# Sort columns of a graph kernel: two-source grids replaced by one-source compares, column by column

## The reference

```
agg  = zeros(N, D).at[src].add(edge_attr)            # layer 0: a sum of edge rows by src
h    = relu(layernorm(x));  x = x + MLP([h, agg, attention(h, u)])
ht   = relu(relu(layernorm(x)) @ W1 + b1)            # layer 1
msg  = sigmoid(exp(w) * ht[src] + b)
fsum = segment_sum(msg, dst, N)                      # a sum of table rows (by src) by dst
out  = x + relu(normalise([ht, c(fsum)] @ Wn + bn))
```

## Time and profile before

| what | us |
|---|---|
| median of three executions | 2619.27 |
| span of the profiled execution | 2625.3 |
| DVE busy | 1911.2 (4995 instructions) |
| PE busy | 1974.8 |
| POOL busy | 1754.5 (1674 instructions) |
| DVE on line 1186, on line 1190 (two groups), on line 1182 (two groups) | 171.7, 166.4 + 165.9, 75.4 + 75.0 |

### The profile page before, as it was taken

How to read it: one execution, slowest core, us unless ns; L and a number is a source line. 1 busy time by engine, 2 the same in 40 slices (tenths; PEclk the granted TensorE clock), 3 DMA queues, 4 the chain that set the end, 5 groups by cost and what they waited for, 6 DMA issues and landing times.

```text
span 2625.3 us, 34327 instructions
## 1 busy us (share of the span) xinstructions
PE 1974.8 (75%) x8533; PEld 1372.0 (52%) x8533; DVE 1911.2 (73%) x4995; ACT 1320.0 (50%) x4349; POOL 1754.5 (67%) x1674
## 2 busy tenths in 40 slices
PE   1389974677867977877898676796897797898884
PEld 0256652445544644644587454564564555575553
DVE  1468882776787798788588578688688689663478
ACT  0145523444744743754436644564564474474565
POOL 1468887777777777777105777777777777777503
PEclk9689986788988998988999798999898999898998
DMA  9989978734643333333365543343333333344445
GB/s 380 280 176 194 195 136 193 179 100 112 163 118 101 107 99 101 105 101 101 106 200 209 180 119 99 111 113 109 111 112 109 110 111 112 111 137 137 118 137 162
DMA packets 182981, 371.10 MB, mean 141 GB/s; under 512 B 33292, under 2 KB 102054, under 8 KB 180213
## 3 DMA queue, kind: packets, MB, share of 16 engines
q0 software_dynamic: 93168, 219.39, 33.8%
q1 hardware_dynamic: 78423, 114.54, 13.5%
q10 hardware_dynamic: 11200, 35.00, 3.5%
HBM read 282.15 MB, written 99.74 MB: 145 GB/s over the span
## 4 chain that ended last, share of the span: by engine, by line
PE 41%; DVE 17%; DMA 12%; POOL 11%; issue 11%; ACT 4%; SPq 3%; DVEq 1%; ACTq 0%; POOLq 0%
PE bank L1514 39%; POOL store L703 10%; DVE agg L1259 7%; DMA store<-in_edge_attr,idx_all 5%; DMA store<-g_table,idx_all 4%; SPq L483 1%; DMA w1bT<-turned_scratch 1%; DVE hits L1186 1%; DVE cum L1143 1%; DVE store L1450 1%; ACT dist L834 1%; POOL agg_copy L677 1%; DMA agg<-in_x 1%; ACT oh L842 1%; ACT store L776 1%
## 5 line engine op out<-in xcount | busy, mean ns | idle before, releaser
L1514 PE MATMUL bank<-store,oh 128*128 (+2 forms) x4610 | 1253.5, 410 | 397.1 <-DMA store<-in_edge_attr,idx_all 115.9
L1514 PEld LDWEIGHTS bank<-store,oh 128*128 128x128 f32 (+1 forms) x4610 | 814.0, 192 | 732.7 <-issue 434.2
L1259 DVE TENSOR_TENSOR agg<-bank,agg 128x256 f32 x1845 | 773.4, 419 | 397.5 <-PE bank L1514 305.9
L703 POOL DMA_INDIRECT store<-g_table,idx_all x785 | 769.4, 980 | 245.9 <-issue 156.3
L842 ACT ACTIVATE oh<-dist 128x128 f32<-128x128 f32 x1845 | 494.7, 302 | 653.9 <-PE bank L1514 628.2
L703 POOL DMA_INDIRECT store<-in_edge_attr,idx_all x628 | 626.0, 997 | 194.3 <-issue 131.3
L834 ACT ACTIVATE dist<-iota,nloc_all 128x128 f32<-128x128 f32 x1845 | 583.1, 387 | 61.8 <-DVE nloc_all L1231 61.8
L677 POOL DMA_INDIRECT agg_copy<-agg x160 | 262.1, 1638 | 154.7 <-ACT agg L799 64.9
L1186 DVE TENSOR_TENSOR hits<-iota,ttab 125x628 f16<-125x628 f16 x360 | 171.7, 477 | 0.0
L1190 DVE TENSOR_TENSOR oh<-hits,v 125x628 f16<-125x628 f16 x360 | 166.4, 479 | 3.2
L1190 DVE TENSOR_TENSOR store<-hits,v 125x628 f16<-125x628 f16 x360 | 165.9, 480 | 3.3
(11 more groups left out here) (211 smaller groups left out, 1926.0 us busy)
## 6 DMA issues: line engine op xcount, KB each, us to landing
agg_copy<-store ACTq DMA_DIRECT2D x4, 6400.0 KB, 38.3
agg<-in_edge_attr SPq DMA_DIRECT2D x39, 512.0 KB, 5.0
agg_copy<-agg_copy POOLq DMA_DIRECT2D x16, 800.0 KB
store<-g_table,idx_all POOLq DMA_INDIRECT x785
store<-in_x SPq DMA_DIRECT2D x48, 256.0 KB, 4.7
store<-in_edge_attr,idx_all POOLq DMA_INDIRECT x628
pre_scratch<-store SPq DMA_DIRECT2D x25, 256.0 KB, 5.3
agg<-agg_copy SPq DMA_DIRECT2D x25, 256.0 KB, 6.8
```

Of the source, the lines that this page charges most:

```text
L703: gp.indirect_dma_start(out=store[:, at % RING * D:(at % RING + 1) * D], out_offset=None, in_=table_dram, in_offset=bass.IndirectOffsetOnA ...
L1259: dve.tensor_tensor(to, pt[n % TB][:, 0:D], to, ALU.add).wait_op(s_mm, n + 1, "sem-ge").then_inc(s_acc, 1)
L1514: return pe.matmul(o, l, r, start=start, stop=stop, skip_group_check=skip)
```

## The change

`COLUMN_OPS` goes from 4 to 3. `hit` is made by four `tensor_scalar` instructions, one per column (a row `counting` of 0, 1, 2, ... in f16 compared with one number per partition from `rtab`). The grid `tile_of` and its semaphore go: each half of `placed` is made by four `tensor_scalar` instructions, which compare `counting` with the partition's `ttab` and multiply with the partition's value in the same instruction. So a batch is 12 instructions of 128 or 158 columns in place of 4 of 512 or 628. The columns lie one behind the other, 158 (`TPAD`) apart, so that PE reads them without stride; buffers move accordingly. Since the column part has 120 atoms in place of 160 at the same planned weight, `spread_over` deals all atoms out anew over the same 146 steps and 40 blocks.

```diff
--- before.py
+++ after.py
@@ -54,6 +54,7 @@
 LOADS = 8
 NLOC = 160
 BOTH = NLOC + TILES
+TPAD = TILES + 1
 TREST = TILES - P
 TURN = 512 - P
 RING = 64
@@ -66,7 +67,7 @@
 
 BATCH = 4
 BATCHES = COLS // BATCH
-COLUMN_OPS = 4
+COLUMN_OPS = 3
 COUNT_ATOM = SEGS
 CC_ATOM = COUNT_ATOM + 3
 PLACE_ATOM = CC_ATOM + 5
@@ -165,6 +166,7 @@
         msk = sb("msk", [P, NWS * COLS], F16)
         cum = sb("cum", [P, NWS * COLS], F16)
         hits = sb("hits", [P, BATCH * TILES], F16)
+        counting = sb("counting", [P, TPAD], F16)
         hit1 = sb("hit1", [P, BATCH * P], F16)
         win = sb("win", [P, SORTS * COLS], F16)
         v1 = sb("v1", [P, SORTS * COLS], F16)
@@ -238,11 +240,10 @@
         ohv = oh[:, 0:OHS * SW].rearrange("p (k n) -> p k n", n=SW)
         distv = dist[:, :].rearrange("p (k n) -> p k n", n=SW)
         columns16 = oh[:, OHS * SW:].bitcast(F16)
-        hit = (columns16[:, 2 * BATCH * TILES:2 * BATCH * TILES + BATCH * P], hit1)
-        tile_of = hits
+        hit = (columns16[:, 2 * BATCH * TPAD:2 * BATCH * TPAD + BATCH * P], hit1)
         spare = store[:, RING * D:].bitcast(F16)
-        placed = tuple(t[:, 0:2 * BATCH * TILES].rearrange("p (v n) -> p v n", v=2) for t in (spare, columns16))
-        after = RING * D + BATCH * TILES
+        placed = tuple(t[:, 0:2 * BATCH * TPAD].rearrange("p (v n) -> p v n", v=2) for t in (spare, columns16))
+        after = RING * D + BATCH * TPAD
         jobtile = store[:, after:after + JT]
         pick = store[:, after + JT:after + 3 * JT].rearrange("p (a n) -> p a n", a=2)
         turned = store[:, after + 3 * JT:after + 3 * JT + 2 * P].rearrange("p (a n) -> p a n", a=2)
@@ -321,7 +322,7 @@
                                                      ("s_mask", "s_colcount", "s_colstart", "s_startstore", "s_startload"))
         s_pf, s_pfd = sem("s_prefix"), sem("s_placed")
         s_col, s_colmm, s_scat, s_dec = (sem(n) for n in ("s_col", "s_colmm", "s_scat", "s_dec"))
-        s_hit, s_code, s_lag = sem("s_hit"), sem("s_code"), sem("s_lag")
+        s_code, s_lag = sem("s_code"), sem("s_lag")
         s_node, s_pick, s_turn, s_nl = (sem(n) for n in ("s_node", "s_pick", "s_turn", "s_jobbias"))
         s_g = [sem(f"s_rows{b}") for b in range(SLOTS)]
         s_abs, s_oh, s_mm, s_acc = (sem(n) for n in ("s_abs", "s_oh", "s_mm", "s_acc"))
@@ -995,6 +996,7 @@
             dve.wait_ge(s_gi, CONSTS)
             pc.mark(dve.tensor_copy(iota1[:, :], dec_a[:, 0:SW]))
             pc.mark(dve.tensor_copy(iota2[:, :, :], dec_a[:, 0:JT].unsqueeze(2).to_broadcast([P, JT, 2])))
+            pc.mark(dve.tensor_copy(counting[:, :], dec_a[:, 0:TPAD]))
             pc.mark(dve.tensor_copy(iotac[:, :], dec_b[:, 0:2]))
             pc.mark(ts(low[:, :], tri[:, :], -1.0, 1.0, ALU.mult, ALU.add))
             pc.mark(dve.tensor_copy(ident16[:, :], ident[:, :]))
@@ -1166,29 +1168,18 @@
                 at = sig * BATCHES + batch
                 b = at % 2
 
-                def pairs(tab, c0):
-                    t = tab[K, c0 + batch * BATCH:c0 + (batch + 1) * BATCH].rearrange("p (a i) -> p a i", i=2)
-                    return lambda width: t.unsqueeze(2).to_broadcast([KP, BATCH // 2, width, 2])
-
-                def grid(t, width):
-                    return t.rearrange("p (a n i) -> p a n i", a=BATCH // 2, i=2)
-
-                def numbers(width):
-                    return iota2[K, 0:width, :].unsqueeze(1).to_broadcast([KP, BATCH // 2, width, 2])
-
+                c0 = batch * BATCH
                 if op == 0:
                     if at >= 2:
                         dve.wait_ge(s_colmm, at - 1)
-                    dve.tensor_tensor(grid(hit[b][K, :], P), numbers(P), pairs(rtab, 0)(P), ALU.is_equal)
-                elif op == 1:
-                    if at:
-                        dve.wait_ge(s_col, at)
-                    dve.tensor_tensor(grid(tile_of[K, :], TILES), numbers(TILES), pairs(ttab, 0)(TILES), ALU.is_equal).then_inc(s_hit, 1)
+                    for i in range(BATCH):
+                        ts(hit[b][K, i * P:(i + 1) * P], counting[K, 0:P], rtab[K, c0 + i:c0 + i + 1], None, ALU.is_equal)
                 else:
-                    v = op - 2
-                    dve.wait_ge(s_hit, at + 1)
-                    r = dve.tensor_tensor(grid(placed[b][K, v, :], TILES), grid(tile_of[K, :], TILES), pairs((v1, v2)[v], sig * COLS)(TILES),
-                                          ALU.mult)
+                    v = op - 1
+                    by = (v1, v2)[v][:, sig * COLS + c0:sig * COLS + c0 + BATCH]
+                    for i in range(BATCH):
+                        r = ts(placed[b][K, v, i * TPAD:(i + 1) * TPAD], counting[K, :], ttab[K, c0 + i:c0 + i + 1], by[K, i:i + 1],
+                               ALU.is_equal, ALU.mult)
                     if v:
                         r.then_inc(s_col, 1)
 
@@ -1617,14 +1608,9 @@
                 b = at % 2
                 pe.wait_ge(s_col, at + 1)
 
-                def column(t, a, i):
-                    return t.rearrange("p (a n i) -> p a n i", a=BATCH // 2, i=2)[:, a, :, i]
-
                 both = pS[:, 0:2 * NLOC].rearrange("p (v n) -> p v n", v=2)[:, :, 0:TILES]
-                for a in range(BATCH // 2):
-                    for i in range(2):
-                        r = mm(both, column(hit[b][K, :], a, i),
-                               placed[b][K, :, :].rearrange("p v (a n i) -> p v a n i", a=BATCH // 2, i=2)[:, :, a, :, i], False, False, True)
+                for i in range(BATCH):
+                    r = mm(both, hit[b][K, i * P:(i + 1) * P], placed[b][K, :, i * TPAD:i * TPAD + TILES], False, False, True)
                 r.then_inc(s_colmm, 1)
 
             def sort_atom(sig, a):
```

## The result

The changed kernel takes 2819.37 us (median of 4 runs, 2817.83 to 2830.08) against 2619.32 for the kernel before on the same chip: ratio 1.0777, 95% interval [1.0758, 1.0797]. It is slower, as forecast, but by 200 us and not by 100.

The account below looks back on a forecast made before the run. POOL's gathers bound the kernel before; after, DVE bounds the column parts. Six groups +84, groups 0 and 4 +16, adding DMAs -10, prologue +10: together +100 on 2619, say 2720 us, range 2620 to 2900.

Parts of the forecast that it names:

- `placed` at 0.17 us: DVE's batch: each of eight `placed` instructions costs 0.17 us, 1.37 us together, within 2.02 us a batch.
- The dearer reading: `placed`: second number per partition costs like the first, 2.54 us a batch; as rival (or no f16 gain) 2880 us, chance 0.18.
- The stall of 0.18 us per gather: Column parts: one-source DVE instructions wait for POOL, 0.18 us charged per gather, bounds 0 and 0.36.
- `hit` at 0.16: DVE's batch: each of four `hit` instructions costs 0.16 us, 0.65 us together.
- the f16 column at half price: DVE instructions: an f16 column costs half of an f32 column's 0.5 ns, so 128 columns take 0.03 us, 158 take 0.04.
- The gathers' excess: Gathers beside columns take 0.994 us, not 0.945; up to 32 us over eight sorts could come back.
- Prologue +10: Prologue: DVE gets 15 us more work and the last blocks are dense, costing 10 us, bounds -8 and +30.
- The order of atoms that I had charged nothing: LAG 5: PE's matmuls one atom behind the `hit` that waits for them; up to 3 us at a time, in the range only.
- The 7 us that I took off each group: Each group: the ring takes up about 7 us of the column part's 27 us excess over POOL's pace.
- The "-10" for the adding DMAs of groups 0 and 1: Groups 0 and 1: 16 adding DMAs that POOL issues now lie beside DVE's work, taking 10 us off.
- The rival "no stall": Column parts: instructions slip between POOL's, groups stay at 203 us, only the prologue counts: 2628 us, chance 0.12.
- a new releaser: Sign at POOL: gathers wait several us for PE, where such waits had been 0.3 us at the longest.

Follow-up runs that it names:

- The strip beside gathers: Strips of twelve DVE instructions per form behind the changed kernel's end, in quiet and beside 40 more gathers: 24 two-number instructions took 5.16 us quiet, 5.19 beside gathers.
- the version whose DVE isn't the bound: Changed kernel with planned column atom weight 0.56 for 0.42 and the second half of `placed` not computed: 2606.30 us, ratio 0.9936 to the kernel before.
- the pair with LAG 4: LAG 4 in place of 5 in the changed kernel and in the kernel before, second chip: 3004.29 us (ratio 1.0460) and 2874.73 us (1.0000).

## Why the prediction was off

Right in sign and in its main mechanism (DVE becomes the bound in the column parts and POOL waits), too small by half. Two large terms of the sum failed, in opposite directions, and a cost that I had put at nothing was not nothing.

- **`placed` at 0.17 us: wrong, 0.232.** This is the step that failed. I put the second number at nothing and gave instructions with two numbers the fixed part of 0.13 us that I had for one. The dearer reading stood among the bounds and the rivals; "both could be fetched together" was all that spoke against it. A batch is 2.51 us and not 2.02; over 320 batches beside gathers that is 157 us of DVE. What taking it away gives back was measured on the third chip alone: 114 and 115 us.
- **The stall of 0.18 us per gather: not in the chain.** In the sum it was 74 x 0.18 = 13 us in six groups and 82 x 0.18 = 15 in two, 109 us in all. The strip beside gathers lost 0.03 us in 24 instructions. Rows 10 and 11 are right for `dec_c`, which is int32 of 160 columns: its chain did get longer (from its start to the next one's 0.35 us at 724.78, inside a gather, and 0.16 us for the `dec_c` at 1533.6, which starts just after one). I carried that over to short f16 instructions, and 522 ns for one of them is a longer duration without a longer chain. Why the two differ, no run shows.
- **`hit` at 0.16: right** (0.162), and so are the f16 column at half price and the split into a fixed part and columns.
- **The gathers' excess: three quarters gone**, from the earlier trace rows; it gave 44 us in the version whose DVE isn't the bound.
- **Prologue +10: it was +28**, within the bounds of that term. The order of atoms that I had charged nothing costs about 25 us there (461.5 to 436.5 us). I had written that late DVE hides it; in the prologue DVE isn't late between the blocks. DVE's additional work costs what is left, 431.2 - 427.1 = 4 us by the pair with LAG 4.
- **The lead that POOL gains in a group is paid at the stage's end.** The 7 us that I took off each group were not measured by themselves. DVE's adds after the last gather of the first stage, 60 us from there on, are the sum rows of six windows of 10 us: 22.47 us of adds before, 28.35 us after, one row from each kernel.

```profile
sum 60.00, DVE 22.47; mean DVE 3.75
```

```profile
sum 60.00, DVE 28.35; mean DVE 4.73
```

The backlog is 28.35 - 22.47 = 5.9 us of adds longer and goes at some 0.57 us a step, in which an add is 0.41: about 8 of the 11.4 us between the stages. The rest of that wasn't followed up.

The recorded working with 2.51 us a batch and no stall: a headed group takes 100.4 + 74 x 0.34 + 83 x 1.25 - 7 = 222 us, 20 more than 202, and groups 0 and 4 take 100.4 + 82 x 0.34 + 75 x 1.25 - 7 = 215, 13 more. Together that is 148 us, against 59.8 + 91.9 = 151.7 in the two stages. With the prologue's 28 and the 11 between the stages it is 187, against 190.7 us between the spans. The "-10" for the adding DMAs of groups 0 and 1 isn't in this; no run shows it, and with it the sum would be 177. (The rival "no stall" was given as 2628 us. It keeps every group at 202 or above and leaves that -10 out; by the terms of the sum it would be 2612.)

What happened was two rivals together, the dear number and no stall, and that pair I hadn't summed. That 2819 still lies inside my range is in part luck: the stall that was missing, 109 us, made up for most of the 157.

Of the signs that I had named, DVE busy throughout (119.00 of 119 us), gathers near 0.95 us and a new releaser came; the distance of two `placed` was the rival's, and a group takes 225 us and not 214 to 218.

The Trainium skill's rule on DVE (VectorE: DVE Perf Modes, "The TRN2 errata"), which I set against the earlier trace rows, gives as an estimate (58 + 158 / 4) / 0.96 = 0.102 us, near the 0.111 of the strip without a number. For such instructions the trace agrees; with one or two numbers the strips show 0.172 and 0.233. By the Trainium skill's lock on the shared ports (SBUF — State Buffer, "Who interferes with whom") whoever starts first keeps them and the other waits for the whole instruction. The single waits up to 0.522 us agree with that, but the chain of these short instructions got only 0.03 us longer and the gathers kept their distance.

## What to carry to other kernels

Count the operands read per partition: an instruction of 158 columns that costs 0.11 us without them costs 0.23 with two, so cutting one wide operation into columns pays only while the numbers are cheaper than the columns saved. Where two unknown costs stand in one sum, work out their combinations too, not each alone against the likeliest. An instruction's duration doesn't tell what it costs in a row of such instructions; read that from start to start, in the form that the change will use. And when the number of pieces in a batch changes, go again through every distance that is counted in pieces (LAG here); look where the late engine that hides it isn't late.

## What was not expected of the hardware

Gathers whose 128 indices all name one row held the DMA queue for 69.7% of 16 engines' time, for 31.0% with the same packets and bytes spread over rows, and the kernel took 3293 us.

On two of the three chips the same kernel took 2874 us and not 2620. The granted TensorE clock, as a share of full speed over the whole span, was 0.902 in the kernel before on the first chip (span 2625.3 us) and 0.862 with LAG 4, which has ratio 1.000, on the second (span 2878.2 us).

In the last group, which has no sort beside it, the changed kernel had PE busy for 177.31 of 198 us at a clock of 0.95 on the first chip, and for 192.79 of 228 us at 0.88 on the third, while the gathers themselves kept their time (147.81 and 147.97 us):

```profile
2470.00:2668.00 198.00, 177.31 (x706) 131.27 (x704) 91.61 (x217) 123.84 (x467) 147.81 (x157) 0.95 0.48 138
```

```profile
2650.00:2878.00 228.00, 192.79 (x683) 133.59 (x684) 87.16 (x207) 117.09 (x441) 147.97 (x157) 0.88 0.40 118
```

On these chips POOL waits for PE even in the kernel before, up to 3.5 us at a time where 0.3 was the longest on the first chip, and for releasers that the profile calls "remote", which the first chip doesn't show at all. These are its waits with LAG 4 on the second chip:

```profile
POOL store L703 <- PE bank L1514: 247.8, 353, 3.5
POOL store L703 <- remote: 100.7, 68, 4.6
```

That part of DVE's additional work hides behind such waits, so that the changed kernel costs 1.056 there and not 1.078, fits these rows but isn't shown by a run of its own. Why the clock is lower on these chips, what "remote" stands for, and whether the two explain all of the longer distances, no run shows.
